# Signs of the attention projections in the weights, the keys' bias in an extra weight row

## What is computed

```
h  = layernorm(x) * (1 + ca) + sa
q  = h @ Wq + bq                                  # 16 heads of 8
lat = gelu(h @ Wkd + bkd)                         # 64 wide
kv = (lat[:, :32] + lat[:, 32:]) @ Wku + bku      # keys 128 wide, values 128 wide
p  = softmax(causal(q @ k.T / sqrt(8)))
x  = x + ga * ((p @ v) @ Wo + bo)
```

## Time and profile before

| | |
|---|---|
| time, median of 3 runs | 689.29 us (688.93 to 690.18) |
| profiled execution, its own time | 689.78 us |
| its span, first to last instruction | 688.0 us |
| mean granted TensorE clock | 0.945 |
| units of the attention in the trace | about 47 to 202 us |

### The profile page before, as it was taken

One profiled execution on the slowest core, in us unless ns is written; L12 is line 12 of the kernel. 1 busy time (PEld: TensorE's weight loads), 2 busy tenths in 40 slices (PEclk: granted clock), 3 DMA queues, 4 the chain that ended last, 5 costly groups with the idle time before them and its releaser, 6 DMA issues.

```text
span 688.0 us, 11080 instructions
## 1 busy us (share of the span) xinstructions
PE 618.3 (90%) x3284; PEld 440.3 (64%) x3284; DVE 547.7 (80%) x1346; ACT 495.5 (72%) x857; POOL 171.3 (25%) x143
## 2 busy tenths in 40 slices
PE   7789989898997899999999999773699899999996
PEld 4455555555543658888888888442375688888884
DVE  3657888888866657888888896855899789999997
ACT  5448999999744559999999999578546366666663
POOL 4212222222401505435554453220142100000000
PEclk9779999999997799999999999997599799999998
DMA  7000000000010040222022210000000032222201
GB/s 236 1 0 1 2 2 1 0 0 0 1 31 0 0 159 0 92 93 86 7 91 91 91 59 26 23 1 0 0 1 0 1 110 107 86 99 85 84 1 61
DMA packets 6653, 29.85 MB, mean 43 GB/s; under 512 B 890, under 2 KB 1027, under 8 KB 4419
## 3 DMA queue, kind: packets, MB, share of 16 engines
q1 hardware_dynamic: 6612, 29.37, 12.0%
HBM read 28.18 MB, written 1.19 MB: 43 GB/s over the span
## 4 chain that ended last, share of the span: by engine, by line
PE 72%; DVE 18%; ACT 5%; issue 3%; DMA 1%; POOL 0%; DVEq 0%; SPq 0%; ACTq 0%; POOLq 0%
PE PS L1117 16%; PE PS L1118 16%; PE PS L1119 16%; DVE STAT L791 5%; PE PS L1236 3%; PE PS L1198 3%; PE PS L1218 3%; PE PS L1232 2%; PE PS L1197 2%; PE PS L1263 2%; PE PS L1143 2%; PE PS L1272 2%; DVE HN L646 2%; PE PS L1130 1%; ACT RA L595 1%
## 5 line engine op out<-in xcount | busy, mean ns | idle before, releaser
L927 DVE TENSOR_TENSOR RA<-AR,RA 128x512 fp32r<-128x512 f32 x140 | 134.3, 983 | 29.2 <-ACT RA L499 28.4
L498 ACT ACTIVATE AR<-PS,BI 128x512 f32<-128x512 f32 x144 | 99.5, 691 | 26.4 <-PE PS L1119 16.6
L1117 PE MATMUL PS<-HH,WH 128*128 128x512 f32 x272 | 109.7, 403 | 0.2
L1118 PE MATMUL PS<-HH,WL 128*128 128x512 f32 x272 | 107.5, 395 | 0.0
L1119 PE MATMUL PS<-HL,WH 128*128 128x512 f32 x272 | 107.3, 395 | 0.0
L499 ACT ACTIVATE RA<-PS,BI 128x512 fp32r<-128x512 f32 x144 | 98.3, 683 | 0.0
L791 DVE CUSTOM_DVE_ANT_0 STAT<-PS,MQ 128x128 f32<-128x128 f32 (+1 forms) x256 | 76.3, 355 | 22.3 <-PE PS L1219 21.8
L1117 PE MATMUL PS<-RA,WH 128*128 128x512 f32 x208 | 82.4, 396 | 2.5 <-DVE RA L1083 2.0
L1119 PE MATMUL PS<-RA,WH 128*128 128x512 f32 x208 | 81.2, 391 | 0.0
L1118 PE MATMUL PS<-RA,WL 128*128 128x512 f32 x208 | 81.2, 390 | 0.0
L303 POOL TENSOR_TENSOR AR<-AR 128x512 f32<-128x512 f32 x32 | 51.1, 1598 | 112.0 <-DVE AR L746 112.0
(11 more groups left out here) (189 smaller groups left out, 1207.3 us busy)
## 6 DMA issues: line engine op xcount, KB each, us to landing
AR<-comb SPq DMA_DIRECT2D x16, 1024.0 KB, 4.6
WS<-in_w SPq DMA_DIRECT2D x9, 512.0 KB, 5.4
WS<-in_w SPq DMA_DIRECT2D x8, 384.0 KB, 3.1
M<-in_mats SPq DMA_DIRECT2D x1, 1384.0 KB, 10.8
X<-in_xT SPq DMA_DIRECT2D x4, 256.0 KB, 4.2
out_xT<-X SPq DMA_DIRECT2D x4, 256.0 KB, 2.1
AR<-in_wmod SPq DMA_DIRECT2D x1, 768.0 KB, 7.7
KM<-in_kmats SPq DMA_DIRECT2D x1, 160.0 KB, 8.3
```

Source lines behind the costliest of these rows:

```text
L498: act.activation(G[:, c, :], PS[:, c, :], ACT.Gelu_apprx_tanh, bias=bias).then_inc(s["act"], 1)
L927: dve.tensor_tensor(out=GL[:, m0 % 2, c, :], in0=G[:, c, :], in1=f(GH[:, m0 % 2, c, :]), op=ALU.subtract).then_inc(s["lo"], 1)
L1117: pe.matmul(out, wh, xh, start=first, stop=False)
L1118: pe.matmul(out, wl, xh, start=False, stop=False)
```

## The change

The signs of `QKR` go into the weights: at the start POOL multiplies the query weights' parts 0, 2 and 3 and the key weights' parts 0, 1 and 3 by -1 (four instructions in place, ahead of `LH` and `LL`), and `join` subtracts in place of adding. `KM` gets a 65th row that holds the keys' bias, `LAT` a 65th row of ones, set by DVE at the very start. `evac_proj` then reads four per-partition operands for its four copies, not eight, and the last two have the function Copy, not Identity. PE waits for the four flips and the row of ones before its first projection. The contraction of L1198 (the keys) and of the 16 matmuls for the values (L1302) is over 65 rows, not 64. The keys' bias and sign leave the vectors, and DVE prepares two columns of biases, not four.

```diff
-        KM = sb("KM", [64, 640])
+        KM = sb("KM", [65, 640])
...
-        LAT = AR[0:64, 8192:10240]
+        LAT = AR[0:65, 8192:10240]
...
+            gp.wait_ge(in_k, 16)
+            km = KM[:, 0:512].rearrange("p (h r c) -> p h r c", r=4, c=8)
+            gp.tensor_scalar(km[:, :, 0:2, :], km[:, :, 0:2, :], -1.0, 0.0, ALU.mult, ALU.add).then_inc(flipped, 1)
+            gp.tensor_scalar(km[:, :, 3, :], km[:, :, 3, :], -1.0, 0.0, ALU.mult, ALU.add).then_inc(flipped, 1)
             gp.wait_ge(in_mats, 16)
+            qm = M[:, MAT_AT["wq"]:MAT_AT["wq"] + 512].rearrange("p (h r c) -> p h r c", r=4, c=8)
+            gp.tensor_scalar(qm[:, :, 0, :], qm[:, :, 0, :], -1.0, 0.0, ALU.mult, ALU.add).then_inc(flipped, 1)
+            gp.tensor_scalar(qm[:, :, 2:4, :], qm[:, :, 2:4, :], -1.0, 0.0, ALU.mult, ALU.add).then_inc(flipped, 1)
...
-                gp.tensor_tensor(out=QKX[:, n % 4, :, :], in0=QKT[:, :, :], in1=f(QKR), op=ALU.add)\
+                gp.tensor_tensor(out=QKX[:, n % 4, :, :], in0=QKT[:, :, :], in1=f(QKR), op=ALU.subtract)\
...
-                for i, name in enumerate(("q", "k")):
-                    act.activation(QKT[:, i, :], PS[:, 6, 256 * i:256 * i + 256], ACT.Identity,
-                                   bias=KEPT[:, i, g:g + 1], scale=vec(name + "_keep")).then_inc(qk_evac, 1)
-                    act.activation(QKR[:, i, :], PS[:, 6, 256 * i:256 * i + 256], ACT.Identity,
-                                   bias=SIGNED[:, i, g:g + 1], scale=vec(name + "_sign")).then_inc(qk_evac, 1)
+                act.activation(QKT[:, 0, :], PS[:, 6, 0:256], ACT.Identity,
+                               bias=KEPT[:, g:g + 1], scale=vec("q_keep")).then_inc(qk_evac, 1)
+                act.activation(QKR[:, 0, :], PS[:, 6, 0:256], ACT.Identity,
+                               bias=SIGNED[:, g:g + 1]).then_inc(qk_evac, 1)
+                act.activation(QKT[:, 1, :], PS[:, 6, 256:512], ACT.Copy, scale=vec("k_keep")).then_inc(qk_evac, 1)
+                act.activation(QKR[:, 1, :], PS[:, 6, 256:512], ACT.Copy).then_inc(qk_evac, 1)
...
+            dve.memset(LAT[64:65, :], 1.0).then_inc(latent_one, 1)
             dve.wait_ge(in_vec, 16)
...
+            pe.wait_ge(latent_one, 1)
+            pe.wait_ge(flipped, 4)
             project(0, 0, 0)
...
-        kmats=np.concatenate([wk, wk]),
+        kmats=np.concatenate([wk, wk, np.concatenate([bk.reshape(1, 512), np.zeros((1, 128), f4)], 1)]),
```

More of the change, by code:

```diff
@@ L12 @@
 MASKED = -1e30
-VECS = dict(bo=1, bq=4, bk=4, q_sign=1, q_keep=1, k_sign=1, k_keep=1, b1=4 * E0, pb=4, gb=3, fb=3,
+VECS = dict(bo=1, bq=4, q_sign=1, q_keep=1, k_keep=1, b1=4 * E0, pb=4, gb=3, fb=3,
             outb=1, alpha=1, norm=1, norm2=1, bkd=1, c=16, prio=8)
@@ L105, in build @@
         QKT = sb("QKT", [128, 2, 256])
-        KEPT = sb("KEPT", [128, 2, 4])
-        SIGNED = sb("SIGNED", [128, 2, 4])
+        KEPT = sb("KEPT", [128, 4])
+        SIGNED = sb("SIGNED", [128, 4])
         NM = sb("NM", [128, 8])
@@ L152, in build @@
         bias_done = sem("bias_done")
+        flipped = sem("flipped")
+        latent_one = sem("latent_one")
         p1_psum, p1_done, a_done, sa_done, hsi_done, sqrt_done, s_ready, scan_done, hs2_mul, hs2_done = map(
@@ L411, in _ @@
                 act.wait_ge(kd_done, t + 1)
-                act.activation(LAT[:, t * BLK:(t + 1) * BLK], PS[0:64, t, :], ACT.Gelu, bias=vec("bkd")[0:64, :])\
+                act.activation(LAT[0:64, t * BLK:(t + 1) * BLK], PS[0:64, t, :], ACT.Gelu, bias=vec("bkd")[0:64, :])\
                    .then_inc(lat_done, 1)
@@ L418, in evac_proj @@
                 if isinstance(n, int) and n == 0:
-                    act.wait_ge(qk_bias, 4)
+                    act.wait_ge(qk_bias, 2)
                 act.wait_ge(proj_done, n + 1)
@@ L860, in step @@
                     attended(n0 - 29)
[L862 to L865, removed]
+            bias = V[:, VAT["bq"]:VAT["bq"] + 4]
+            dve.tensor_scalar(KEPT[:, :], bias, vec("q_keep"), None, ALU.mult).then_inc(qk_bias, 1)
+            dve.tensor_scalar(SIGNED[:, :], bias, vec("q_sign"), -1.0, ALU.mult, ALU.mult).then_inc(qk_bias, 1)
             dve.wait_ge(sp_done, 3)
@@ L1581, in layouts @@
     put("bq", heads(a["L0_attn_bq"], 3).T)
-    put("bk", bk.T)
     put("q_sign", np.array([1, -1, 1, 1], f4)[row])
     put("q_keep", np.array([0, 1, 0, 0], f4)[row])
-    put("k_sign", np.array([1, 1, -1, 1], f4)[row])
     put("k_keep", np.array([0, 0, 1, 0], f4)[row])
```

## The result

The changed kernel takes 678.62 us (median of 4, 677.29 to 680.24), the kernel before 689.11 beside it: ratio 0.9853 [0.9816, 0.989]. A second measurement, with its own runs of the kernel before, gave 677.21 and 0.9827 [0.9811, 0.9842]. Predicted were 682.9 us and a range of 679.8 to 687.3: the direction is right, the gain is 4 us larger than forecast, and the time is 1.2 us under the range's lower end.

A forecast was written before the change was run, and what follows sets the result against it. Bound: the attention step's chain over PE and DVE, 4.72 us. Steps -5.6, start's copies -0.74, projections -0.6, flips +0.5 sum to -6.4 from 689.78: 683.4, less 0.5 to the median: 682.9 us, range 679.8 to 687.3.

The forecast's parts named there:

- PE on the chain, ACT hidden: Attention steps: chain runs over PE and DVE only; ACT has 0.32 us slack, so cheaper copies gain steps nothing.
- The form costs 0.20 and 0.15 us: PE at L1198 and L1272: entering the 64-row form costs 0.20 us, leaving 0.15; 65 rows remove both, 0.35 per step.
- rival 2: L1198's operands, not the form, cause the gaps; 65 rows close nothing, only the start changes: 689.0 us, chance 0.08.
- How much of 0.35 us the step gains is DVE's to say: Attention steps: DVE's room limits the gain to 0.24 us without L832, 0 with it; steps 0 to 2 gain 0.35.
- DVE caps the step: Main case, attention steps: form changes but DVE limits the gain; 682.9 us, own range 680.5 to 686.0, chance 0.78.
- rival 3: ACT or PE alone sets the step, DVE having more slack: 11.0 to 12.2 us less, 677.1 to 678.3, chance 0.07.
- The start: -0.84 predicted: Before the attention steps: shorter copies -0.74, second and third projections' form -0.6, POOL's flips +0.5 us.
- Theory C: Whole kernel, a theory set up for the experiments: what is unexplained comes from the clock; no size or chance given.
- The flips on POOL: At the start, flips of M ahead of L273 and L275 delay the chain by 0.5 us, between -0.3 and +0.95.
- The clock, rival 4: Start changes delay the clock's rise, so steps run at half clock: slower, +0.5 us or +4 (693), chance 0.07.
- The profiled execution against the median: Whole kernel: the profiled execution, 689.78 us, was taken as 0.5 us above the median of 689.29.

The follow-up runs named there:

- Experiment 2: Kernel before with only the four cheaper ACT copies, still 64 rows, no flips, signs and keys' bias left out: 686.88 us, ratio 0.9965.
- experiment 1: Kernel before with only the 65th rows added to KM (zeros) and LAT (ones), copies keeping all eight operands: 680.47 us, ratio 0.9854.
- Experiment 5: Kernel before with three extra unused 128-element DVE copies in each of 19 steps without L832: 689.05 us, ratio 0.9996.
- experiment 7: Changed kernel with POOL's weight work moved behind DVE's normalisation and the values' copies moved from DVE to POOL: 674.02 us, ratio 0.9779.
- experiment 4: Changed kernel with one extra unused 128-element DVE copy in each of 19 steps without the values' copies: 680.44 us, ratio 0.985.
- experiment 3: Changed kernel without POOL's four flips and the wait for them, signs left out: 677.19 us, ratio 0.9819.

## Why the prediction was right in sign and too small

- **PE on the chain, ACT hidden: right.** Experiment 2 takes 0.36 us from ACT in each step and the step stays at 4.73.
- **The form costs 0.20 and 0.15 us: right.** They are there with 64 rows (experiment 2: 0.63 and 0.37) and gone with 65, signs or no signs (experiment 1), and 64 rows between 64 rows cost nothing (L1302). L1198's operands were still `LAT` and `KM` there, so rival 2 is out. The Trainium skill, "TensorEngine Tiling (Array Packing)", section Key Properties, says that changing the tiling mode drains the engine; the times agree, 0.20 and 0.15 us at the two changes. The trace shows the late weight load and not the drain.
- **"How much of 0.35 us the step gains is DVE's to say": the step that failed, by its size.** The prediction counted DVE's room as the pause between L817 and L811, 0.26 us, and none in steps with L832. It took L811 to L791 (0.44 us) as work without a pause. Experiment 5 measures 0.36 us of room, the other 0.11 lying just there: L791 waited for PE's scores, which stand behind the transposes on PE. So steps without L832 gained 0.34 and not 0.24 (19 x 0.10 = 1.9 us), and those with L832 gained 0.10 and not 0 (7 x 0.10 = 0.7 us): 2.6 of the 2.8 us by which the steps missed. With these two values the sum of steps is 3 x 0.35 + 19 x 0.34 + 7 x 0.10 = 8.2 us, and 8.4 were measured.
- **DVE caps the step: right with L832, wrong without.** With the two copies DVE sets the step: taken off it, 4.62 falls to 4.39 (experiment 7). Without them the chain is drawn over DVE, but its room of about 0.02 us (experiment 4) puts it level with PE's path, 4.72 less 0.35, 4.37: PE's gain arrives almost in full. ACT is not far either: with its old copies it is nearly without a wait at 4.39 (experiment 1). So in steps without L832 rival 3's arithmetic (the full 0.35) was as good as true. Its reason does not carry where L832 stands: there DVE keeps 0.25 of the 0.35. That its total of 677.1 to 678.3 lies close to the measured 678.62 is in part luck: it had 10.2 us or more from the steps, which gave 8.4, and the start and the spread between executions made up for it.
- **The start: -0.84 predicted, -1.4 measured, by a mix that was not foreseen.** Up to the first of the four copies it is 2.3 us later (31.16 for 28.87): the modulation vectors came 1.5 us later in this execution, and 0.75 is more than the 0.5 given to the flips. Behind that it is 3.7 us shorter, where 1.34 was predicted. The copies gave 0.36 in each of the two groups, 0.37 was predicted; the projections gave 1.24 each time and not 0.30, because in addition to the form the clock was higher; scores and clock matmuls gave the other 0.5. Windows of the changed kernel:

```profile
33.00:36.00 3.00, 2.32 (x15) 1.58 (x14) 1.18 (x9) 0.11 (x1) 1.14 (x1) 1.00 0.00 0
...
40.00:41.00 1.00, 1.00 (x4) 0.71 (x3) 0.00 (x0) 0.53 (x2) 0.32 (x1) 0.50 0.00 0
41.00:42.00 1.00, 1.00 (x6) 0.47 (x4) 0.00 (x0) 0.00 (x0) 0.95 (x1) 0.50 0.00 0
42.00:43.00 1.00, 0.68 (x4) 0.43 (x4) 0.96 (x2) 0.00 (x0) 0.00 (x0) 0.76 0.00 0
```

  The kernel before has 0.50 from 33 to 36 us:

```profile
33.00:36.00 3.00, 3.00 (x10) 1.50 (x8) 1.80 (x9) 0.51 (x2) 0.00 (x0) 0.50 0.00 0
```

  The fall to 1.2 GHz moved behind the second projection, and the rise still falls at 42 to 43 us. From the first copies to the second it is 4.73 us (31.16 to 35.89) and was 6.62 (28.87 to 35.49): 1.9 us less, for 0.67 predicted. Where the fall comes is not a property of the kernel alone: experiment 5, whose instructions up to there are those of the kernel before, takes 5.28 us for that stretch, with a granted clock of 1.00 up to 36 us. Why it moved is open. Theory C has its place here and only here.
- **The flips on POOL: 0.5 us predicted, 0.62 measured on POOL** (1.12 in the first profile, where the first flip took 0.79 beside DVE's L652). Whether they reach the end is not shown (experiment 3).
- **The clock, rival 4: did not happen.** The granted clock is 1.00 from 44 us to the end of the steps in both kernels. At the start the clock helped, which the prediction allowed for only as a width of 1.7 us.
- **The profiled execution against the median:** 1.2 us above it here, 0.5 before. These 0.7, 2.8 of the steps, 0.5 of the start and 0.3 of the rest are the 4.3 us by which the forecast was too high. The range was missed by 1.2 us; the 2.6 us of DVE's room alone would have put the forecast at 680.3, inside it.

## What to carry to other kernels

A start-to-start distance on an engine is work only if it appears just as long where the engine is known to be held up by nothing; compare the same pair in a place where the engine is late, or add a harmless operation ahead and see how much of it arrives. When a gap closes on the bounding engine, count the next engine's room over its whole segment up to the point where it releases the first, since each pause in it shrinks. And a contraction with fewer rows can cost more than one with a few more, if its neighbours run in the other form; between its own kind it does not.

## What the runs showed of the hardware that was not expected

- A 65-row float32 matmul between 128-row ones takes 0.43 us for two passes of 256 columns, a 64-row one 0.63 plus 0.15 us for the matmul behind it, at 2.4 GHz (experiments 1 and 2). The weight load of the 64-row one waited 0.33 us and began only as the matmuls ahead of it ended. 29 passes of 128 columns in a row take 3.40 us with 64 rows and with 65.
- POOL's operations at the start hold even tiny ones on DVE for their whole length (3.67 us for 128 x 32 elements). It goes the other way too: POOL's flip of 128 elements took 0.79 us in the execution where it started at 16.36, beside DVE's L652 (16.30 to 16.99), and 0.30 in the other.
- DVE's copy of the modulation vectors starts between 13.67 and 16.12 us in the twelve profiled executions; in three kernels with the same instructions ahead of it (before, experiments 2 and 5) it starts at 13.67, 16.10 and 15.49. The part behind the attention differs by 2.8 us between two executions of one kernel (502.5 and 499.7), and lies between 498.2 and 502.8 in the eight profiles where its instructions are the same. Both are more than several terms of the prediction.
